# One maximum over both halves of a score group in a ViT block's window attention

## The reference

```
hd = C // NH                                   # 8 heads of 8
xw = x in windows of 8 x 8 tokens              # 256 windows of 64 tokens
qkv = xw @ qkv_w.T + qkv_b
q, k = _rope2(q), _rope2(k)                    # rotary encoding by row and column
attn = softmax(q * scale @ swapaxes(k, -2, -1), axis=-1)   # 64 x 64 scores per window and head
out = (attn @ v)                               # back to (B, H*W, C)
h = out @ proj_w.T + proj_b
h = h + scan(layernorm(h))
h = h + experts(layernorm(h))
```

## Time and profile before

| | |
|---|---|
| median of 3 runs | 658.89 us (656.12 to 661.49) |
| the profiled execution, its own time | 659.24 us |
| its span in the trace | 657.2 us |
| what lies around the span | 2.04 us |
| granted TensorE clock, mean | 0.945 |
| TensorE, VectorE, ScalarE, GpSimd busy | 566.3, 526.6, 404.3, 308.4 us |
| attention in the trace, first to last maximum (L661) | 73.2 to 313.0 us |

### The profile page before, as it was taken

How to read it: one execution, slowest core, us unless ns; L and a number is a source line. 1 busy time by engine, 2 the same in 40 slices (tenths; PEclk the granted TensorE clock), 3 DMA queues, 4 the chain that set the end, 5 groups by cost and what they waited for, 6 DMA issues and landing times. The chain is left out here.

```text
span 657.2 us, 18275 instructions
## 1 busy us (share of the span) xinstructions
PE 566.3 (86%) x7079; PEld 385.3 (59%) x7080; DVE 526.6 (80%) x943; ACT 404.3 (62%) x659; POOL 308.4 (47%) x352
## 2 busy tenths in 40 slices
PE   3795499999999999999955666649999999999995
PEld 3331388888888888888721222235555555555552
DVE  3898389999889999989669899957777777777762
ACT  3696267767777777777759556504555555555543
POOL 5401234555555565555299759853433333332420
PEclk9899599999999999999967888978999999999998
DMA  9500222223322222221000000000011010101001
GB/s 194 84 1 9 61 56 51 54 55 65 72 57 55 51 56 52 59 55 28 2 0 1 0 0 0 2 1 10 21 22 23 21 24 20 25 19 23 22 21 25
DMA packets 62376, 23.01 MB, mean 35 GB/s; under 512 B 45778, under 2 KB 62290, under 8 KB 62290
## 3 DMA queue, kind: packets, MB, share of 16 engines
q1 hardware_dynamic: 61472, 21.69, 16.1%
q10 hardware_dynamic: 690, 0.13, 0.1%
q0 software_dynamic: 128, 0.00, 0.0%
HBM read 5.02 MB, written 4.19 MB: 14 GB/s over the span
## 5 line engine op out<-in xcount | busy, mean ns | idle before, releaser
L602 ACT ACTIVATE work<-work 128x1024 f32<-128x1024 f32 x64 | 67.7, 1057 | 66.3 <-DVE work L666 66.3
L661 DVE TENSOR_REDUCE work<-psum 128x16 f32<-128x1024 f32 x64 | 78.0, 1219 | 30.1 <-PE psum L502 30.1
L469 POOL TENSOR_TENSOR work<-work 128x4 f32<-128x4 f32 x32 | 34.3, 1072 | 105.3 <-DVE work L703 105.3
L517 PE MATMUL psum<-kc,work 128*128 128x128 f32 x512 | 75.2, 280 | 8.9 <-DVE work L678 7.8
L666 DVE TENSOR_TENSOR work<-psum,work 128x1024 f32<-128x1024 f32 x64 | 78.3, 1224 | 2.2
L1724 ACT ACTIVATE hid<-psum,b1c 128x512 f32<-128x512 f32 x96 | 58.9, 684 | 33.3 <-PE psum L1631 33.3
L610 ACT ACTIVATE work<-psum 128x512 f32<-128x512 f32 x128 | 71.0, 591 | 6.4 <-PE psum L517 4.9
L1639 PE MATMUL psum<-x_t,w1x 64*64 64x256 f32 x1024 | 71.7, 396 | 0.0
L517 PEld LDWEIGHTS psum<-kc,work 128*128 128x128 f32 x512 | 58.4, 143 | 17.4 <-DVE work L678 15.5
L1614 POOL TENSOR_TENSOR m_sq<-m_xc 128x256 f32<-128x256 f32 x32 | 19.6, 612 | 101.5 <-DVE m_xc L1775 101.5
L533 PEld LDWEIGHTS psum<-work 128*64 128x64 f32 x2048 | 62.3, 138 | 6.2 <-ACT work L610 6.0
(11 more groups left out here) (192 smaller groups left out, 1260.1 us busy)
## 6 DMA issues: line engine op xcount, KB each, us to landing
work<-big_bc SPq DMA_DIRECT2D x256, 32.0 KB, 2.0
h_all<-in_x SPq DMA_DIRECT2D x16, 256.0 KB, 5.2
work<-big_a SPq DMA_DIRECT2D x32, 128.0 KB, 2.2
out<-out_st SPq DMA_DIRECT2D x128, 32.0 KB
w1x<-in_L_ffn_W SPq DMA_DIRECT2D x2, 128.0 KB, 4.3
kc<-constants SPq DMA_DIRECT2D x1, 202.0 KB, 2.9
w2x<-in_L_ffn_W SPq DMA_DIRECT2D x1, 128.0 KB, 3.2
wraw<-in_L_tok_qkv_w ACTq DMA_DIRECT2D x2, 32.0 KB, 3.6
```

The lines of the kernel that those rows point to most:

```text
L469: pool.tensor_tensor(rstd[:, :], var[:, :], mhalf[:, :], ALU.pow).then_inc(rstd_done, 1)
L517: m = pe.transpose(banks[4 + half][:, n * P:n * P + P], prob[:, f, at:at + 2, :], ident)
L602: act.activation(prob[:, f], prob[:, f], ACT.Exp).then_inc(prob_done, 1)
L661: dve.tensor_reduce(top[:, f, :].rearrange("p (g h) -> p g h", g=4), sc, AX.X, ALU.max).then_inc(top_done, 1)
```

## The change

`lower(i)` now handles both halves of a group. One `tensor_reduce` over all four banks in full gives the 32 maxima (128 x 2048 in, 128 x 32 out, over a pattern of four nested dimensions: half, bank, run, element), then the two subtractions follow, half 0 first. `top_done` counts one a group. The subtractions, their waits for `turned` and their `low_done` stay. All that depends on `low_done` is as it was; TensorE, ScalarE, GpSimd and SyncE have the same instructions in the same order.

```
-        def lower(i, f):
+        def lower(i):
 
-            sc = psum[:, 0:4, f * 256:f * 256 + 256].rearrange("p g (h k) -> p g h k", k=WIN)
+            sc = psum[:, 0:4, :].rearrange("p g (f h k) -> p f g h k", f=2, k=WIN)
             dve.wait_ge(scores_done, i * 4 + 4)
-            dve.tensor_reduce(top[:, f, :].rearrange("p (g h) -> p g h", g=4), sc, AX.X, ALU.max).then_inc(top_done, 1)
-            dve.wait_ge(top_done, i * 2 + (f + 1))
+            dve.tensor_reduce(top[:, :, :].rearrange("p f (g h) -> p f g h", g=4), sc, AX.X, ALU.max
+                              ).then_inc(top_done, 1)
+            dve.wait_ge(top_done, i + 1)
+            for f in range(2):
+                if not first(i):
+                    dve.wait_ge(turned, i * 4 + (2 * f - 2))
+                dve.tensor_tensor(prob[:, f].rearrange("p (g h) k -> p g h k", g=4), sc[:, f],
+                                  top[:, f, :].rearrange("p (g h) -> p g h", g=4).unsqueeze(3).broadcast_to([P, 4, 4, WIN]),
+                                  ALU.subtract).then_inc(low_done, 1)
 
         def body(i, par):
             if live(i, -1):
-                lower(i + 1, 0)
-                lower(i + 1, 1)
+                lower(i + 1)
                 copy_v(i + 1, 1 - par)
```

## The result

The changed kernel takes 652.47 us (median of 6 runs, 650.07 to 653.53) against 657.85 for the kernel before (6 runs, 655.83 to 661.49): a ratio of 0.9914, with a 95% interval of 0.9886 to 0.9941. The forecast was 653.7 us, 0.8% less. Its profiled execution took 652.73 us, with a span of 650.7.

The account below looks back on a forecast made before the run. A VectorE–TensorE loop of 7.61 us a group was taken as the bound; removing 2.51 and adding 2.34 saves 0.17, 31 x 0.17 - 0.06 = 5.2 us, 658.89 to 653.7 us. Range 650.8 to 658.4.

Parts of the forecast that it names:

- The bound: Attention groups: a loop through VectorE and TensorE, score operations 4.79, copies 0.92, second half-turn 0.58, scores 1.32, sets the 7.61 us period.
- The maximum: VectorE, each group: one merged maximum of 2048 elements takes 2.30 us (2.29 to 2.33).
- the slower rival: Merged maximum on VectorE: its four-dimensional pattern runs at half pace, 4.42 us, 62 us longer in all; chance 0.05.
- The hand-over: VectorE, between the merged maximum and the subtraction waiting for it: 0.04 us, with the subtractions 1.14 apart.
- The rival that a hand-over is worth nothing: VectorE score operations: merging saves only fixed cost, 0.07 us a group, 2.2 us in all, 656.7; chance 0.14.
- What is late next: Attention: half 0's exponential, 1.08 us later, stays covered with 0.12 to spare; TensorE is the next limit, 0.24 away.
- sign of no wait for the exponential outside the first group: Profile after: TensorE waits for the exponential (L602) before its first four transposes only in the first group.
- The first group: First attention group, at 1.2 GHz: the late exponential of half 0 makes it lose 0.06 us in place of gaining 0.17.
- the 1.05 us for four transposes at 1.2 GHz: First group on TensorE: four transposes and the step to the scores take 1.05 us, so the second four start at 78.95.
- The sum: Whole kernel: 31 x 0.17 - 0.06 = 5.2 us saved, 653.7 us, 0.8% faster.
- the forecast's 31st group: Last attention group: its turn precedes the scan's first matmuls on TensorE, so it passes on its 0.17 us gain.

Follow-up runs that it names:

- The pair of kernels with the copies elsewhere: `copy_v` moved from VectorE to ScalarE, between the two exponentials, in the kernel before (646.24 us, ratio 0.9811) and in the changed one (646.80 us, 0.9825).
- the order alone: Kernel before with its two maxima, unmerged, both ahead of the two subtractions: 648.48 us, ratio 0.9846; once more, 649.50 us, ratio 0.9842.
- the repeat: The change itself against the kernel before, measured and profiled once more, beside the kernel with both maxima first on one chip: 651.21 us, ratio 0.9886.
- the kernel with half 1 first: Changed kernel (merged maximum) with the subtraction of half 1 ahead of that of half 0: 678.74 us, ratio to the kernel before 1.0287.

## Why the prediction was right

- **The bound.** The loop maximum, subtraction, copies, second half of the turn, scores was the period, and it is after the change: 2.32 + 2.28 + 0.92 + 0.58 + 1.32 = 7.42. The pair of kernels with the copies elsewhere shows that the loop goes through the copies: with those off VectorE, merging gains nothing.
- **The maximum.** Taken at 2.30, bounds 2.29 to 2.33; it is 2.292. The slope from 1024 to 2048 elements is (2292 - 1219) / 1024 = 1.048 ns. A fourth dimension in the pattern has no price here, so the slower rival had nothing.
- **The hand-over.** Taken as 0.04 behind the maximum (measured 202.81 - 200.49 - 2.29 = 0.03), with subtractions 1.14 apart (2.28 / 2). The rival that a hand-over is worth nothing is refuted by the order alone: 0.26 us a group with no instruction less. The Trainium skill ("VectorE: DVE Perf Modes", The DRAIN you can't avoid) reports that a chain of eight copies took the same time with a semaphore after each as with one after the last. That does not carry over to a VectorE instruction that waits for the one directly ahead of it: in this kernel that costs 0.13. The prediction split the saving into 0.08 of fixed cost and 0.1 of hand-over; the runs give 0.07 and 0.13.
- **What is late next.** The wait for the copies was to fall from 0.40 to 0.23 and is 0.21, and TensorE's own period was put 0.24 below the new one; the kernel with copies on ScalarE runs at 7.23, 0.19 below. The exponential of half 0 did not bind at the full clock, though in the second group, where TensorE has no projection to do yet, it waited 1.0 us for it ahead of the first four transposes, which the prediction had only for the first group. The row of the waits from 82 to 310 us in the changed kernel:

```profile
PEld psum L517 <- DVE work L679: 7.3, 31, 0.4
...
PEld psum L517 <- ACT work L602: 1.0, 1, 1.0
```

  The copies came later all the same: TensorE waited 0.41 us for them there, before its second four, so it cost nothing. So the prediction's sign of no wait for the exponential outside the first group failed in the second. In the repeat that wait is 1.5.
- **The first group** was put at a loss of 0.06 and gained 0.10 (81.70 - 72.81 = 8.89 against 82.18 - 73.19 = 8.99). The step that failed: the 1.05 us for four transposes at 1.2 GHz was the distance from the second four to the scores, which holds a wait of 0.33 that the first four don't have. The row shows eight loads in 1.57 us and 1.90 from the first to the scores:

```profile
77.57 1.57 PEld L517 LDWEIGHTS psum<-kc,work 128*128 128x128 f32 x8 [2.32 <-ACT work L602]
...
79.47 1.80 PEld L502 LDWEIGHTS psum<-work 32*128 32x128 f32 x32 [0.33 <-issue]
```

  Up to the scores the gain is in both profiles of the changed kernel: 79.47 - 72.81 = 6.66 us, and 78.16 - 71.51 = 6.65 in the repeat, against 79.94 - 73.19 = 6.75 before. The whole group is no measure of the change: in the repeat it took 8.53, with a mean clock of 0.59 from the transposes' loads to the next maximum (76.20 to 80.04) in place of 0.50 (77.57 to 81.70), and shorter loads for the scores:

```profile
78.16 1.53 PEld L502 LDWEIGHTS psum<-work 32*128 32x128 f32 x32 [0.33 <-issue]
```

- **The sum.** 5.2 us were forecast and 5.8 are found in the groups (5.71 + 0.10): 0.02 a group from rounding the terms, and the first group; the forecast's 31st group, the last, lies in the 0.31 behind them. The median moved by 5.4. That it came within 0.2 of the forecast is in part luck: in the repeat the same change moved it by 7.7. What stands behind the account is the period, 7.44 forecast and 7.42 in both profiles.

The merge was valued rightly, but the better change lay beside it: moving one instruction, without merging, saves 0.26 us a group where the merge saves 0.19.

## What to carry to other kernels

Where one in-order engine does pairs of producer and consumer, write the independent producers first and the consumers behind: each direct hand-over taken out saved 0.13 us here, and the order took out both. Merging two producers into one took out one hand-over and 0.07 of an operation's fixed part, and left the other hand-over. Before counting on either, follow the loop to the instruction that the other engine truly waits for (here the copies behind the subtractions): when that one moved to another engine, the same edit was worth nothing. And a merge delays the first consumer: have the margin of whoever reads the first half before you make it.

## What the runs showed of the hardware that was not expected

One short stall of TensorE was followed by a lower clock, and the two together cost three times the stall's length. In the kernel before with copies on ScalarE, all periods behind the first are 6.94 to 7.23 us, but one is 9.79. There a transfer of tokens was issued at 152.70, among those of the experts' weights, and TensorE waited 0.83 us for it, until 156.66. Windows of the group ahead, of that group, of the stretch behind the stall, and of the next group (columns as in the earlier trace rows):

```profile
145.19:152.41 7.22, 7.22 (x144) 6.67 (x143) 6.02 (x8) 6.38 (x13) 4.22 (x6) 1.00 0.27 59
152.41:162.20 9.79, 9.05 (x144) 8.24 (x143) 6.02 (x8) 6.93 (x14) 4.25 (x6) 0.83 0.37 60
156.60:161.40 4.80, 4.74 (x48) 4.34 (x52) 1.90 (x5) 2.87 (x5) 1.01 (x1) 0.64 0.26 51
162.20:169.43 7.23, 7.23 (x144) 6.68 (x143) 6.02 (x8) 6.07 (x11) 4.17 (x5) 1.00 0.45 74
```

The weight loads of the same kernel there:

```profile
156.66 0.55 PEld L566 LDWEIGHTS psum<-w_v,work 128*64 128x64 f32 x16 [0.83 <-DMA work<-big_a]
157.27 1.68 PEld L574 LDWEIGHTS psum<-w_out,work 72*128 72x128 f32 x8
```

The granted clock fell to a mean of 0.64 behind the stall, so for most of that stretch to the level of 1.2 GHz, and the eight loads of the projection took 1.68 us in place of 0.97. Of the 2.56 us that the group was longer, 0.83 is the wait. From the projection's loads to the scores' it is 3.61 us (160.88 - 157.27) in place of 1.97 (204.25 - 202.28), so 1.64 goes with the clock. Waits of 0.4 and 0.2 us in every group left the clock at 1.00 in the kernel before and after.

But a wait of that length does not bring the clock down each time. In the kernel with half 1 first, TensorE waits 0.91 us or more for the exponential in every group of the attention. Two windows of one group each, and the loads behind the wait in the second of them:

```profile
175.22:183.39 8.17, 7.45 (x144) 6.71 (x143) 6.71 (x10) 5.48 (x11) 4.19 (x5) 1.00 0.32 70
183.39:193.16 9.77, 9.05 (x144) 8.15 (x143) 6.71 (x10) 5.78 (x11) 4.19 (x5) 0.83 0.25 53
...
189.21 1.50 PEld L517 LDWEIGHTS psum<-kc,work 128*128 128x128 f32 x8 [0.91 <-ACT work L602]
```

Both have the same wait of 0.91, and only the second has the lower clock, and with it 1.60 us more. From the fourth group on no other period is over 8.17. (In the second group, from 84.01 to 93.55, the wait was 2.61 us and the mean clock 0.83.) What makes one such wait different from the others isn't shown. With the copies off the loop, the transfers of x are the next thing to watch; whether the clock falls at this place in each execution isn't known from one profile.
